# Last stage of a transformer kernel on one core: the gated difference is added into the residual by GpSimd instead of VectorE

## The chip, the cores and the metric

The kernel is one program on one NeuronCore of a Trainium2 chip. Time is device microseconds of that core, and less is better. The engines are TensorE (PE), VectorE (DVE), ScalarE (ACT), GpSimd (POOL) and SyncE (SP), each with its own queue of instructions, and they wait for each other by semaphores that the program sets by hand. Data sits in SBUF, 128 partitions wide; "128x512" is 128 partitions by 512 fp32 elements.

## What is computed

Two pre-norm layers over an input of 4 x 1024 tokens with 128 features: attention, a routed feed-forward, a second attention with fixed offsets, and a last feed-forward with two experts per token. Only the last is touched. Cut to what matters:

```
def _forward(x, ...):
    residual = x
    abel_out = gelu(xn @ abel_w + abel_b)
    topw, topi = top_k(xn @ moe_gate_w + moe_gate_b, 2); topw = softmax(topw)
    moe_out = sum over the two experts of topw * (gelu(xn @ ew1 + eb1) @ ew2 + eb2)
    for i in range(3): moe_out = moe_out @ expm(gens[i])
    gate = sigmoid(concat([abel_out, moe_out]) @ gc_w + gc_b)
    mixed = abel_out * (1.0 - gate) + moe_out * gate
    return residual + mixed
```

The kernel computes the last two lines as residual + abel_out + gate * (moe_out - abel_out). The product with the gate is the "gated difference".

## The kernel before

The residual `x` stays in SBUF for the whole program as 32 tiles of 128 tokens (`[128, 32, 128]`). In the last feed-forward the tokens are sent to their experts' rows in DRAM, 71 tiles of expert rows go through TensorE, and each result row is scattered to `yq` in DRAM by an indirect DMA from POOL (L2132). Beside those tiles, DVE's `pre` steps (L2097 to L2100, one for each of the 32 token tiles) take the gate's share of `ab` (`abel_out`) and add `ab` into `x`.

When all 71 scatters have landed, the part that the change touches begins. The 32 token tiles are taken in eight slices `u` of four tiles. The order of the steps is written out at L1907 to L1913: in turn u come `gate1` of slice u, `mix` of slice u - 1 and `fin` of slice u - 2. Each engine walks that list and does its own part of each step:

- SP loads slice u of `yq` into one of five buffers `yb` (L1947). The first five loads go at once. The later three each wait for the `mix` and the gate sum of the slice whose buffer they take, and stand in SP's queue in turn with the stores (L1951), each of which waits for its slice's `fin`.
- `gate1`: POOL makes the gate's argument in `s0m` with four operations on 128x4 elements (L2142 to L2145), and ACT takes its tanh (L2040).
- `mix`: DVE makes `mo = w0*y0 - ab` (L2111, four operations on 128x128) and `mo = w1*y1 + mo` (L2115, four more), where y0 and y1 are the two experts' rows of `yb`. `mo` has two buffers. POOL turns the tanh into the gate `gt` (L2151). ACT multiplies, `gd = gt * mo` (L2048, four on 128x128). `gd` has two buffers too, so ACT waits for the `fin` of two slices before.
- `fin`: DVE adds `gd` into `x`, one operation on 128x512 (L2121), and signals `v_out`.

`dve.then(ins)` lets DVE wait for its own instruction before the next one. The semaphore names `v_`, `a_`, `g_` and `d_` say who signals: DVE, ACT, POOL or a DMA.

Of the kernel before, what the change touches and what calls it, by code (L numbers as in the profile page):

```python
# [10 lines left out]
ALU = mybir.AluOpType  # L11
# [4 lines left out]
NT = B * T // 128  # L16
# [1785 lines left out]
NX1, NY1, NB1 = 6, 5, 5  # L1802
# [114 lines left out]
def ffn1_sync(p, k, sp, ye):  # L1917
    a = p.a
    ye.dma_start(k.e2T[:], a["e2T"]).then_inc(p.sem("d_f1e").h, 16)
    ye.dma_start(k.b2s[:], a["b2s"]).then_inc(p.sem("d_f1e").h, 16)  # L1920
    ye.dma_start(k.e1[:], a["e1"]).then_inc(p.sem("d_f1e").h, 16)
    sp.wait_ge(p.sem("d_f1"), 16 * len(k.loads))
    ye.dma_start(k.xq[8 * CAP:8 * CAP + 128, :], k.small["pads"][:]).then_inc(p.sem("d_pad").h, 16)
    sp.wait_ge(p.sem("v_end"), 1)
    for e in range(8):
        end = ye.value_load(k.endi[0:1, e:e + 1], min_val=0, max_val=8 * CAP - 128)
        ye.dma_start(k.xq[bass.ds(end, 128), :], k.small["pads"][:]).then_inc(p.sem("d_pad").h, 16)
    sp.wait_ge(p.sem("d_pad"), 16 * 9)
    for q in range(NQ1):
        sp.wait_ge(p.sem(f"d_xq{q}"), 16 * 2 * G * len(range(q, NC1, NQ1)))  # L1930
    sp.wait_ge(p.sem("v_row"), 1)
    for t in range(NE1):
        if t >= NX1:
            sp.wait_ge(p.made("turn1"), t - NX1 + 1)
            sp.wait_ge(p.sem("v_id"), t - NX1 + 1)
        row = ye.value_load(k.rowi[0:1, t:t + 1], min_val=0, max_val=8 * CAP)
        ye.dma_start(k.xg[t % NX1][:], k.xq[bass.ds(row, 128), :]).then_inc(p.sem(f"d_xh{t % NX1}").h, 16)
    for i in range(NY1):
        sp.wait_ge(p.sem(f"d_yq{i}"), 16 * len(range(i, NE1, NY1)))
    o_v = p.out.rearrange("(n p) d -> p n d", p=128)  # L1940
    y_v = k.yq.rearrange("(u p r) d -> u p (r d)", u=8, p=128)
    for u in range(8 + NB1):
        if u < 8:
            if u >= NB1:
                sp.wait_ge(p.sem("v_mo"), u - NB1 + 1)
                sp.wait_ge(p.sem("g_sum"), u - NB1 + 1)
            ye.dma_start(k.y[u % NB1][:].rearrange("p i h d -> p (i h d)"), y_v[u]).then_inc(p.sem(f"d_yb{u % NB1}").h, 16)  # L1947
        if u >= NB1:
            n = 4 * (u - NB1)
            sp.wait_ge(p.sem("v_out"), u - NB1 + 1)  # L1950
            ye.dma_start(o_v[:, n:n + 4, :], p.x[:, n:n + 4, :]).then_inc(p.sem("d_out").h, 16)  # L1951
    sp.wait_ge(p.sem("d_out"), 16 * 8)

# [46 lines left out]
def ffn1_scalar(p, k, act, se):  # L2000
    S = p.S
    cols = k.small["cols"]
    for w in k.items:
        s = w.slot
        if w.kind in R1ACT:
            route1_scalar(p, k.route, act, se, w)
        elif w.kind == "ab":
            c = w.at[0]
            act.wait_ge(p.done("ab"), w.n)
            se.activation(k.ab[:, G * c:G * c + G, :], k.ab[:, G * c:G * c + G, :], ACT.Gelu).then_inc(p.sem("a_ab").h, 1)  # L2010
        elif w.kind == "fold":
            f = w.at[0]
            act.wait_ge(p.made("fold"), w.n)
            se.activation(k.er[:, 774 * f:774 * f + 774].rearrange("p (h n) -> p h n", h=2),
                          S[s][:].rearrange("p (h n) -> p h n", h=2)[:, :, 0:387], ACT.Copy).then_inc(p.done("fold").h, 1)
        elif w.kind == "tiles":
            act.wait_ge(p.sem("v_gap"), NC1)
            se.activation(k.dd[:], k.dd[:], ACT.Tanh, scale=0.5).then_inc(p.sem("a_top").h, 1)
        elif w.kind == "turn1":
            t = w.at[0]  # L2020
            act.wait_ge(p.made("turn1"), w.n)
            if t > 3:
                act.wait_ge(p.made("up1"), t - 3)
            se.activation(k.xT[t % 4][:], S[s][:, 0:128], ACT.Identity, bias=cols[:, 2:3], scale=cols[:, 1:2]).then_inc(p.done("turn1").h, 1)
        elif w.kind == "up1":
            t = w.at[0]
            act.wait_ge(p.made("up1"), w.n)
            act.wait_ge(p.sem("v_w"), w.n)
            if t > 3:
                act.wait_ge(p.made("down1"), t - 3)  # L2030
            for j in range(2):
                c = slice(128 * j, 128 * j + 128)
                ins = se.activation(k.h[t % 4][:, c], S[s][:, c], ACT.Gelu, bias=k.w[t % 4][:, 256 + j:257 + j])  # L2033
            ins.then_inc(p.done("up1").h, 1)
        elif w.kind == "gate1":
            u = w.at[0]
            act.wait_ge(p.sem("g_sum"), u + 1)
            if u == 0:
                act.wait_ge(p.sem("v_half"), 1)
            se.activation(k.s0[u % 2][:], k.s0[u % 2][:], ACT.Tanh, bias=cols[:, 0:1], scale=0.5).then_inc(p.sem("a_gate").h, 1)  # L2040
        elif w.kind == "mix":
            u = w.at[0]
            act.wait_ge(p.sem("v_mo"), u + 1)
            act.wait_ge(p.sem("g_gate"), u + 1)
            if u > 1:
                act.wait_ge(p.sem("v_out"), u - 1)
            for i in range(4):
                ins = se.activation(k.gd[u % 2][:, i, :], k.mo[u % 2][:, i, :], ACT.Identity, scale=k.gt[u % 2][:, i:i + 1])  # L2048
            ins.then_inc(p.sem("a_gd").h, 1)


def ffn1_vector(p, k, dve, ve):
# [9 lines left out]
    for w in k.items:  # L2062
# [21 lines left out]
        elif w.kind == "up1":  # L2084
            t = w.at[0]
            dve.wait_ge(p.sem(f"d_xh{t % NX1}"), 16 * (t // NX1 + 1))
            if t > 7:
                dve.wait_ge(p.sem(f"d_yq{(t - 8) % NY1}"), 16 * ((t - 8) // NY1 + 1))
            ve.tensor_copy(k.id[t % 8][:], k.xg[t % NX1][:, 128:129]).then_inc(p.sem("v_id").h, 1)
        elif w.kind == "down1":  # L2090
            t = w.at[0]
            dve.wait_ge(p.made("down1"), w.n)
            if t >= NY1:
                dve.wait_ge(p.sem(f"d_yq{t % NY1}"), 16 * (t // NY1))
            ve.tensor_tensor(k.yo[t % NY1][:, 0:129], A[s][:, 0:129], k.er[:, bass.ds(expert[t] * 129 + 16 * 129, 129)], ALU.add).then_inc(p.done("down1").h, 1)  # L2095
        elif w.kind == "pre":
            n = w.at[0]  # L2097
            dve.wait_ge(p.sem("a_ab"), n // G + 1)
            ve.tensor_tensor_reduce(k.junk[:], k.ab[:, n, :], sm["gca"][:], 1.0, 0.0, ALU.mult, ALU.add, k.sA[:, n:n + 1])
            dve.then(ve.tensor_tensor(x[:, n, :], x[:, n, :], k.ab[:, n, :], ALU.add))  # L2100
        elif w.kind == "mix":
            u = w.at[0]
            mo, y = k.mo[u % 2], k.y[u % NB1]
            dve.wait_ge(p.sem(f"d_yb{u % NB1}"), 16 * (u // NB1 + 1))
            if u == 0:
                dve.wait_ge(p.sem("a_ab"), NC1)
            if u > 1:
                dve.wait_ge(p.sem("a_gd"), u - 1)
            for i in range(4):
                n = 4 * u + i  # L2110
                ins = ve.scalar_tensor_tensor(mo[:, i, :], y[:, i, 0, 0:128], k.w01[:, 0, n:n + 1], k.ab[:, n, :], ALU.mult, ALU.subtract)  # L2111
            dve.then(ins)
            for i in range(4):
                n = 4 * u + i
                ins = ve.scalar_tensor_tensor(mo[:, i, :], y[:, i, 1, 0:128], k.w01[:, 1, n:n + 1], mo[:, i, :], ALU.mult, ALU.add)  # L2115
            ins.then_inc(p.sem("v_mo").h, 1)
        elif w.kind == "fin":
            u = w.at[0]
            xc = x[:, 4 * u:4 * u + 4, :]
            dve.wait_ge(p.sem("a_gd"), u + 1)  # L2120
            ve.tensor_tensor(xc, xc, k.gd[u % 2][:], ALU.add).then_inc(p.sem("v_out").h, 1)  # L2121


def ffn1_gpsimd(p, k, pool, ge):
    for w in k.items:
# [20 lines left out]
        elif w.kind == "mix":  # L2146
            u = w.at[0]
            pool.wait_ge(p.sem("a_gate"), u + 1)
            if u > 1:
                pool.wait_ge(p.sem("a_gd"), u - 1)  # L2150
            ge.tensor_scalar(k.gt[u % 2][:], k.s0[u % 2][:], 0.5, 0.5, ALU.mult, ALU.add).then_inc(p.sem("g_gate").h, 1)  # L2151

# [2 lines left out]
def program(nc, a, out):  # L2157
# [28 lines left out]
    for i in range(4):  # L2186
        p.again(f"d_yq{i}", f"d_ys{i}", 16 * len(range(i, NE, 4)))
    p.again("d_xq0", "d_sc0", 16 * NT)
    for new, old, n in (("v_id", "a_near", NT), ("v_w", "a_far", NT), ("v_mo", "v_sub", NT), ("g_sum", "v_far", NT), ("v_out", "g_lt", NT),
                        ("a_gd", "v_gate", NCH), ("a_gate", "g_bo", NCH), ("g_gate", "v_add", NT), ("v_pos", "a_ex", 2 * B), ("v_oh", "v_hot", 2 * B),  # L2190
                        ("a_n2", "v_negmax", 2 * B)):
        p.again(new, old, n)
# [165 lines left out]
```

## Time and profile before

| | us |
|---|---|
| median of 3 runs | 1600.14 |
| lowest, highest | 1599.58, 1601.69 |
| the profiled execution's own time | 1601.15 |
| its span in the trace | 1599.4 |
| from `yb` landed (first L2111) to the end of the last L2121 | 1573.11 to 1596.64 |

The profiled execution lies 1.0 us above the median, and 1.75 us of its time lie outside its span. Times in the rows below count from the start of the span. A row of the timeline gives the start, the duration, the engine, the line, the operation, `out<-in` by the program's names (buffer numbers left out), the shapes and how many such instructions are merged in it. The operations of one engine overlap by some tenths of a microsecond at their ends, so four operations of 0.35 us in a row take 1.06 from the first start to the next operation's start.

### The profile page before, as it was taken

How to read it: one execution, taken by the hardware profiler on the slowest of the kernel's cores; microseconds unless marked ns; L12 is line 12 of the kernel's file. 1: busy time of each engine (PE TensorE's matmuls, PEld its weight loads, DVE VectorE, ACT ScalarE, POOL GpSimd, SP SyncE). 2: the span in 40 equal slices, each digit the busy share in tenths (PEclk: the TensorE clock that was granted, in tenths of full speed). 3: DMA queues.
4: the chain of work that ended last, by engine and by line, in shares of the span. 5: the costliest groups of instructions: out<-in, count | busy, mean ns of one | idle time of the engine just before them, and what ended most of it. 6: DMA issues, size and time to landing. Idle time of an engine off the chain costs nothing.

```text
span 1599.4 us, 37167 instructions
## 1 busy us (share of the span) xinstructions
PE 1296.5 (81%) x13212; PEld 850.4 (53%) x13212; DVE 1159.1 (72%) x3814; ACT 728.2 (46%) x1523; POOL 692.9 (43%) x1004
## 2 busy tenths in 40 slices
PE   3479899898998888989896799948999988666881
PEld 2234444445454454544444576627777776556770
DVE  5568788786888969879764554437899998973556
ACT  1136456454565545555561133414544444215773
POOL 3013232233333333323221123347877888764664
PEclk9679999998999999999996799967987777657995
DMA  4664726557264571745705111102111112032335
GB/s 107 93 102 66 117 42 94 81 85 116 31 105 77 91 115 26 115 72 90 112 3 204 56 33 34 41 24 82 43 43 43 49 49 70 21 118 74 92 97 168
DMA packets 73863, 123.19 MB, mean 77 GB/s; under 512 B 17518, under 2 KB 46067, under 8 KB 72784
## 3 DMA queue, kind: packets, MB, share of 16 engines
q1 hardware_dynamic: 64960, 106.74, 35.2%
q0 software_dynamic: 7616, 13.59, 2.6%
q8 instruction: 108, 1.77, 0.5%
q10 hardware_dynamic: 1104, 0.48, 0.1%
q14 instruction: 75, 0.61, 0.1%
HBM read 30.40 MB, written 17.60 MB: 30 GB/s over the span
## 4 chain that ended last, share of the span: by engine, by line
PE 35%; DVE 26%; POOL 12%; SPq 8%; issue 8%; DMA 5%; ACT 4%; DVEq 1%; POOLq 0%; ACTq 0%
SPq L499 8%; DVE first L779 5%; PE S L1033 5%; PE A L593 4%; POOL xq L1356 4%; DVE S L782 3%; PE S L576 3%; PE S L565 3%; PE S L557 2%; PE A L1045 2%; DVE tA L758 2%; POOL prod L1779 2%; PE S L1546 2%; DVE tB L759 2%; PE S L179 1%
## 5 line engine op out<-in xcount | busy, mean ns | idle before, releaser
L670 ACT ACTIVATE P<-S 128x512 f32<-128x512 f32 (+3 forms) x768 | 332.8, 490 | 281.1 <-PE S L576 276.2
L565 PE MATMUL S<-Kp,Qp 120*128 120x512 f32 (+3 forms) x768 | 253.7, 399 | 48.5 <-issue 15.0
L853 POOL TENSOR_SCALAR_AFFINE_SELECT P<-P 128x256 f32<-128x256 f32 (+1 forms) x256 | 116.9, 460 | 403.0 <-ACT P L670 402.7
L576 PE MATMUL S<-Qp,Kp 121*128 121x512 f32 (+3 forms) x768 | 255.1, 396 | 34.4 <-DVE tB L759 9.8
L782 DVE CUSTOM_DVE_ANT_0 S<-S,later 128x512 f32<-128x512 f32 (+3 forms) x512 | 239.2, 514 | 55.4 <-PE S L565 54.8
L565 PEld LDWEIGHTS S<-Kp,Qp 120*128 120x128 f32 x768 | 134.2, 196 | 182.2 <-issue 71.2
L779 DVE TENSOR_REDUCE first<-S 128x1 f32<-128x512 f32 x256 | 164.4, 683 | 49.2 <-PE S L565 49.0
L576 PEld LDWEIGHTS S<-Qp,Kp 121*128 121x128 f32 x768 | 140.0, 193 | 112.5 <-issue 25.2
L593 PE MATMUL A<-P,V 128*9 128x512 f32 (+3 forms) x1536 | 174.0, 501 | 5.6 <-POOL P L853 5.5
L2132 POOL DMA_INDIRECT yq<-yq,id x71 | 69.4, 978 | 48.6 <-DVE yq L2095 26.2
L1779 POOL TENSOR_TENSOR prod<-qf,kT 128x128 f32<-128x128 f32 x160 | 73.3, 492 | 33.1 <-ACT qf L1614 24.8
L1192 POOL DMA_INDIRECT ys<-yo,id x39 | 38.1, 977 | 106.5 <-DVE yo L1172 102.6
L1356 POOL DMA_INDIRECT xq<-n,posu x64 | 67.3, 1052 | 38.1 <-DVE posu L1340 18.8
L1546 PE MATMUL S<-kT,Qm 32*32 32x64 f32 x4096 | 60.2, 234 | 24.1 <-DVE sc L1707 7.6
L1033 PE MATMUL S<-w,xgT 128*128 x156 | 76.5, 613 | 3.6 <-issue 2.2
L1163 DVE SCALAR_TENSOR_TENSOR uu<-th,S 128x512 f32<-128x512 f32 x39 | 26.8, 688 | 68.0 <-ACT th L1065 68.0
L782 DVE DVE_READ_ACCUMULATOR2_ANT mx<- 128x1 f32 x512 | 71.9, 140 | 0.0
L1546 PEld LDWEIGHTS S<-kT,Qm 32*32 32x32 f32 x4096 | 47.8, 109 | 38.5 <-issue 13.1
L1662 ACT ACTIVATE pt<-S 128x1024 f32<-128x1024 f32 x32 | 32.7, 1022 | 55.5 <-PE S L1563 55.5
L758 DVE TENSOR_TENSOR tA<-S,cos 128x512 f32<-128x512 f32 x60 | 41.2, 686 | 21.9 <-PE S L557 11.7
L1995 PE MATMUL A<-er,hq 128*128 x284 | 51.3, 304 | 4.6 <-issue 2.9
L2083 DVE COPY wq<-e 128x258 f32 x71 | 21.5, 302 | 45.4 <-ACT hq L2033 24.8
(335 smaller groups left out, 2707.6 us busy)
## 6 DMA issues: line engine op xcount, KB each, us to landing
Qp<-rcq SPq DMA_DIRECT2D x64, 256.0 KB
Kp<-rck SPq DMA_DIRECT2D x64, 256.0 KB
Qp<-rcq SPq DMA_DIRECT2D x64, 128.0 KB
Kp<-rck SPq DMA_DIRECT2D x64, 128.0 KB
xq<-xq SPq DMA_DIRECT2D x71, 72.0 KB, 1.9
yb<-yq SPq DMA_DIRECT2D x8, 528.0 KB, 4.4
Qp<-cq SPq DMA_DIRECT2D x64, 64.0 KB
Kp<-ck SPq DMA_DIRECT2D x64, 64.0 KB
```

The lines of the kernel that those rows point to most:

```text
L499: ye.dma_start(rows, src).then_inc(p.sem(f"d_q{u % 4}").h, 16)
L565: te.matmul(S[s][:, 512 * h:512 * h + n], Q[0:120, h, 128 * qt:128 * qt + 128], K[0:120, h, 512 * part:512 * part + n], start=True, stop=T ...
L576: te.matmul(S[s][:, 512 * h + c:512 * h + 512], K[0:121, h, 128 * kb:128 * kb + 128], Q[0:121, h, 512 * qh + c:512 * qh + 512], start=True ...
L593: ins = te.matmul(A[oa][o:o + 9, c:512], k.V[u // 8 % 2][:, kb, 2 * (u % 8) + h, :], k.P[(e.n - 1) % NP0][:, h, c:512], start=kb < 2, stop ...
L670: se.activation(k.P[(w.n - 1) % NP0][:, h, c:512], S[s][:, 512 * h + c:512 * h + 512], ACT.Exp, scale=SCALE0).then_inc(p.done("st").h, 1)
L779: ve.tensor_reduce(k.first[:, h, qt - 4:qt - 3], S[s][:, 512 * h:512 * h + 512], AX.X, ALU.max).then_inc(p.done("mx").h, 1)
L782: ins = ve.tensor_tensor_reduce(out=of, in0=of, in1=k.later[:, 512 - n:512], scale=1.0, scalar=-3e38, op0=ALU.add, op1=ALU.max, accum_out= ...
L853: ge.affine_select(P[:, :, start:c + 128], P[:, :, start:c + 128], [[0, 2], [1, wide]], ALU.is_ge, 0.0, base=start - c, channel_multiplier ...
L1033: ins = te.matmul(S[s][:, c:c + 512], k.xgT[t % NH][:], k.w1[:, bass.ds(expert[t] * 1024 + c, 512)], start=True, stop=True)
L1356: ge.indirect_dma_start(r.xq, bass.IndirectOffsetOnAxis(r.posu[q][:, h, i:i + 1], 0), r.n2[q][h][:, i, :], None).then_inc(p.sem(f"d_xq{q}" ...
L1546: ins = te.matmul(C[32 * q:32 * q + 32, 64 * h:64 * h + 64], k.Qm[c % 2][rows, j, 128 * i + 32 * q:128 * i + 32 * q + 32], k.kT[c % 2][row ...
L1779: ins = ge.tensor_tensor(prod[:, n, :], q, kT[:, at:at + 128], ALU.mult)
```

## The change

`fin` moves from DVE's queue to POOL's, at the same place in the list of steps. POOL waits for `a_gd` of the slice and for `v_pre`, a semaphore that now counts DVE's 32 additions of `ab` into `x` (before, DVE counted them on its own semaphore and waited for itself there; it now waits on `v_pre` instead). POOL's addition signals `g_out`, and the three that waited for `v_out` (SP's store, ACT's `gd` buffer, the semaphore's reuse table) take `g_out`.

```diff
@@ ffn1_sync
         if u >= NB1:
             n = 4 * (u - NB1)
-            sp.wait_ge(p.sem("v_out"), u - NB1 + 1)
+            sp.wait_ge(p.sem("g_out"), u - NB1 + 1)
@@ ffn1_scalar
             if u > 1:
-                act.wait_ge(p.sem("v_out"), u - 1)
+                act.wait_ge(p.sem("g_out"), u - 1)
@@ ffn1_vector
-            dve.then(ve.tensor_tensor(x[:, n, :], x[:, n, :], k.ab[:, n, :], ALU.add))
+            ve.tensor_tensor(x[:, n, :], x[:, n, :], k.ab[:, n, :], ALU.add).then_inc(p.sem("v_pre").h, 1)
+            dve.wait_ge(p.sem("v_pre"), n + 1)
...
-        elif w.kind == "fin":
-            u = w.at[0]
-            xc = x[:, 4 * u:4 * u + 4, :]
-            dve.wait_ge(p.sem("a_gd"), u + 1)
-            ve.tensor_tensor(xc, xc, k.gd[u % 2][:], ALU.add).then_inc(p.sem("v_out").h, 1)
@@ ffn1_gpsimd
+        elif w.kind == "fin":
+            u = w.at[0]
+            xc = p.x[:, 4 * u:4 * u + 4, :]
+            pool.wait_ge(p.sem("a_gd"), u + 1)
+            pool.wait_ge(p.sem("v_pre"), NT)
+            ge.tensor_tensor(xc, xc, k.gd[u % 2][:], ALU.add).then_inc(p.sem("g_out").h, 1)
```

DVE's queue in the stage, from the first `mix` of slice 0, before:

```order
3128 L2111 SCALAR_TENSOR_TENSOR mo<-yb,w,ab 128x128 x4
3129 L2115 SCALAR_TENSOR_TENSOR mo<-yb,w,mo 128x128 x4
3130 L2111 SCALAR_TENSOR_TENSOR mo<-yb,w,ab 128x128 x4
3131 L2115 SCALAR_TENSOR_TENSOR mo<-yb,w,mo 128x128 x4
3132 L2121 TENSOR_TENSOR x<-x,gd 128x512
3133 L2111 SCALAR_TENSOR_TENSOR mo<-yb,w,ab 128x128 x4
```

and after it (two lines further down in the file, L2112 is the old L2111, L2116 the old L2115):

```order
3128 L2112 SCALAR_TENSOR_TENSOR mo<-yb,w,ab 128x128 x4
3129 L2116 SCALAR_TENSOR_TENSOR mo<-yb,w,mo 128x128 x4
3130 L2112 SCALAR_TENSOR_TENSOR mo<-yb,w,ab 128x128 x4
3131 L2116 SCALAR_TENSOR_TENSOR mo<-yb,w,mo 128x128 x4
3132 L2112 SCALAR_TENSOR_TENSOR mo<-yb,w,ab 128x128 x4
```

All eight additions are gone from DVE's queue; its `mix` steps of all slices stand in a row.

POOL's queue at the same place, from the `gt` of slice 0 on, before:

```order
586 L2151 TENSOR_SCALAR gt<-s0m 128x4
587 L2142 TENSOR_TENSOR s0m<-yb,w 128x4
588 L2143 TENSOR_TENSOR s1m<-yb,w 128x4
589 L2144 TENSOR_TENSOR s0m<-s0m,s1m 128x4
590 L2145 TENSOR_TENSOR s0m<-s0m,sA 128x4
591 L2151 TENSOR_SCALAR gt<-s0m 128x4
592 L2142 TENSOR_TENSOR s0m<-yb,w 128x4
```

and after it (here the lines are four lower, L2138 is the old L2142 and L2147 the old L2151):

```order
586 L2147 TENSOR_SCALAR gt<-s0m 128x4
587 L2138 TENSOR_TENSOR s0m<-yb,w 128x4
588 L2139 TENSOR_TENSOR s1m<-yb,w 128x4
589 L2140 TENSOR_TENSOR s0m<-s0m,s1m 128x4
590 L2141 TENSOR_TENSOR s0m<-s0m,sA 128x4
591 L2147 TENSOR_SCALAR gt<-s0m 128x4
592 L2153 TENSOR_TENSOR x<-x,gd 128x512
593 L2138 TENSOR_TENSOR s0m<-yb,w 128x4
```

The addition of slice u stands behind the `gt` of slice u + 1 and in front of the four small operations of slice u + 3.

## Rows read from the trace of the kernel before

**Rows 1.** The page's first part: busy time, share of the span, instructions

```profile
PE 1296.5 (81%) x13212; PEld 850.4 (53%) x13212; DVE 1159.1 (72%) x3814; ACT 728.2 (46%) x1523; POOL 692.9 (43%) x1004
```

**Rows 2.** Windows, the last stage: length, then each engine's busy us (instructions), clock, DMA

```profile
1573.00:1597.00 24.00, 0.00 (x0) 0.00 (x0) 22.50 (x72) 12.17 (x40) 11.75 (x40) 0.50 0.66 225
```

**Rows 3.** The chain that ended last, 1569 to the end: start, us, what

```profile
1569.46 3.62 DMA yb<-yq
...
1573.11 1.15 DVE mo L2111 x4
...
1576.51 1.14 DVE mo L2115 x4
1577.65 0.60 DVE x L2121
1578.25 1.06 DVE mo L2111 x4
...
1591.78 0.60 DVE x L2121
1592.38 1.06 DVE mo L2111 x4
...
1593.47 1.15 DVE mo L2115 x4
1594.64 0.40 ACT gd L2048
...
1595.95 0.69 DVE x L2121
```

**Rows 4.** L2121's own view: ns of one, least, median and most; starts; forms

```profile
L2121 DVE TENSOR_TENSOR x<-x,gd x8: 684/684/691, 1577.6 to 1596.0; 128x512 f32<-128x512 f32 x8
```

**Rows 5.** The same view of L1768, POOL's addition in the stage before

```profile
L1768 POOL TENSOR_TENSOR x<-x,bo x8: 1268/1274/1293, 1070.7 to 1295.6; 128x512 f32<-128x512 f32 x8
```

**Rows 6.** L1714's own view, and one L1714 beside POOL's L1768 in the timeline

```profile
L1714 DVE TENSOR_TENSOR sc<-sc,mx x32: 1307/1309/2257, 1085.2 to 1378.4; 128x1104 f32<-128x1104 f32 x32
...
1142.92 1.68 DVE L1714 TENSOR_TENSOR sc<-sc,mx 128x1104 f32<-128x1104 f32 x1
...
1142.15 1.29 POOL L1768 TENSOR_TENSOR x<-x,bo 128x512 f32<-128x512 f32 x1
```

**Rows 7.** L1682's own view, and one L1682 beside POOL's L1791 in the timeline

```profile
L1682 DVE SCALAR_TENSOR_TENSOR x<-yg,share,x x32: 338/350/2110, 1064.6 to 1265.6; 128x128 f32<-128x128 f32 x32
...
1112.89 0.88 DVE L1682 SCALAR_TENSOR_TENSOR x<-yg,share,x 128x128 f32<-128x128 f32 x1
1112.89 0.72 POOL L1791 TENSOR_TENSOR ls<-lt 128x256 f32<-128x256 f32 x1
```

**Rows 8.** Timeline at 1194: POOL's L1791 beside an L1714 that began before it

```profile
1194.03 1.31 DVE L1714 TENSOR_TENSOR sc<-sc,mx 128x1104 f32<-128x1104 f32 x1
...
1194.17 1.75 POOL L1791 TENSOR_TENSOR ls<-lt 128x256 f32<-128x256 f32 x1
```

**Rows 9.** Timeline of the last stage: POOL's small operations, and one L2121 of DVE

```profile
1573.17 0.36 POOL L2142 TENSOR_TENSOR s0m<-yb,w 128x4 f32<-128x4 f32 x1 [4.84 <-DMA yb<-yq]
...
1574.46 0.23 POOL L2142 TENSOR_TENSOR s0m<-yb,w 128x4 f32<-128x4 f32 x1
...
1577.16 0.28 POOL L2151 TENSOR_SCALAR gt<-s0m 128x4 f32<-128x4 f32 x1
...
1577.57 0.69 DVE L2121 TENSOR_TENSOR x<-x,gd 128x512 f32<-128x512 f32 x1
1577.59 0.72 POOL L2142 TENSOR_TENSOR s0m<-yb,w 128x4 f32<-128x4 f32 x1
```

**Rows 10.** DMAs of the last stage, 1569 to the end: count, KB, median us to landing

```profile
yb<-yq SPq DMA_DIRECT2D x8, 528.0 KB, 4.4
out<-x SPq DMA_DIRECT2D x8, 256.0 KB, 2.3
```

More of the change, by code:

```diff
@@ L2188, in program @@
     p.again("d_xq0", "d_sc0", 16 * NT)
-    for new, old, n in (("v_id", "a_near", NT), ("v_w", "a_far", NT), ("v_mo", "v_sub", NT), ("g_sum", "v_far", NT), ("v_out", "g_lt", NT),
+    for new, old, n in (("v_id", "a_near", NT), ("v_w", "a_far", NT), ("v_mo", "v_sub", NT), ("g_sum", "v_far", NT), ("g_out", "g_lt", NT),
                         ("a_gd", "v_gate", NCH), ("a_gate", "g_bo", NCH), ("g_gate", "v_add", NT), ("v_pos", "a_ex", 2 * B), ("v_oh", "v_hot", 2 * B),
```

## The prediction, made before the changed kernel had run

> **What bounds the kernel now.** I read the page's busy shares first: over the whole span VectorE (DVE) is busy 72% and GpSimd (POOL) 43% [rows 1], which says nothing yet about the stage that is changed. The windows view does: in the 24 us from 1573 to 1597 TensorE is idle, DVE is busy 22.50 us, ACT 12.17 and POOL 11.75 [rows 2]. The stage is DVE's. The chain of waits shows how: after the last scatter the read back of `yb` ends at 1573.11, and from there the chain stays on DVE without a gap, four L2111 (1.06), four L2115 (1.14), one L2121 (0.60 by its place in the chain), and so on [rows 3]. L2121 stands in it six times at 0.60, for the slices (u) 0 to 5; the period is 2.82 us (1.06 + 0.02 issue + 1.14 + 0.60). The end is a tail with three members: the last L2115, then ACT's four products (1594.64 to 1595.92), then the last L2121, 0.69 long, then the last store. So six of the eight adds are on the path before the last `mo`, the seventh (u = 6) lies beside ACT's last products, and the eighth closes the kernel.
>
> **What it removes.** Six adds of 0.60 before the last `mo`: 6 x 0.60 = **-3.6 us**. DVE's step falls from 2.82 to 2.22 us, if nothing holds it.
>
> **The last add.** It changes engine. POOL did an add of the same shape, `x<-x,bo`, 128 x 512 in place, eight times, in 1.27 us [rows 5], against DVE's 0.68 to 0.69 [rows 4]: 1.27 - 0.69 = **+0.58 us** (its second input is one row read four times over, which is the one difference). By the Trainium skill (GPSIMD Engine Reference, section 3.1) a two-input op on GpSimd takes about 1.96 times VectorE's time; that would make the last add 1.35 instead of 1.27, and the row is what I use. The store behind it is unchanged, 2.3 us to landing [rows 10].
>
> **The adds in the middle, and what they hold up.** Here is the term that decides. POOL's add of slice u can start when ACT has written `gd`, 1.34 us after the last L2115 of slice u (1594.62 to 1595.95 at the end), and then DVE is in the middle of slice u + 1, in operations that all have two inputs in SBUF (`yb` and `ab`, `yb` and `mo`). The trace of before has many places where such a DVE operation meets a POOL operation that reads SBUF. Four of them:
> - L1714 takes 1.31 alone. At 1142.92 it took 1.68, and POOL's 128 x 512 add was under way from 1142.15 to 1143.44 [rows 6]. It ended 1.16 us after POOL's end: it had waited for POOL to finish and then streamed its 1104 elements.
> - L1682, an operation of the very kind and shape of L2111, takes 0.35 in the median. At 1112.89 it started together with a POOL add of 256 elements (0.72) and took 0.88, ending 0.16 after POOL's end [rows 7]. It was held for 0.88 - 0.35 = 0.53, which is POOL's 0.72 less 0.19.
> - The other way round: at 1194.17 POOL's 256-element add met an L1714 that had begun at 1194.03, and took 1.75 instead of about 0.72. It ended 0.59 after the DVE operation's end [rows 8].
> - In the stage itself POOL's L2142 on four elements began 0.02 after an L2121 and took 0.72, ending at 1578.31, 0.05 after it [rows 9].
>
> So one waits until the other has done its whole operation. POOL's add gets in behind the L2111 or L2115 that is running, and the next one stands until POOL has finished. The price of one add for DVE, as in the L1682 row: 1.27 - 0.19 = 1.08 us. How many meet DVE: the adds of u = 0 to 6 each start 1.3 to 1.4 us into a DVE step that lasts 2.2 or more, so all seven, u = 6 too, which before lay beside ACT and now falls into the last slice's L2115. 7 x 1.08 = **+7.6 us**. Bounds of this price: back-to-back operations start every 0.265 us (1.06 / 4) and stream their 128 elements in 0.13 (L1714's 1104 in 1.16), so up to 0.13 more may be hidden between two, 0.95 each (6.7); or nothing is hidden, 1.27 each (8.9). I take 1.08, since its row is the same DVE instruction. By the Trainium skill (SBUF — State Buffer, "SBUF: two separate sides") the port pair that both engines share is an exclusive lock: whoever starts first has it "for the whole instruction; the other fully blocks". Taken literally that is 1.27 per add and a sum of +5.9 us; the rows bear out that it is exclusive, and price it 0.19 lower.
>
> POOL's four-element operations stand between DVE's now and cost it nothing visible: the step with them (u = 1 to 6) and the last without them both show 1.06 and 1.14 to 1.15 [rows 3]. I leave them at zero.
>
> **What is queued behind the new waits.** On POOL the add waits for `a_gd`. Behind it in POOL's order are the four small operations of slice u + 3 and the `gt` of slice u + 2. A block of four takes 1.29 from start to start, and `gt` 0.3 [rows 9]. So POOL's step is 1.29 + 0.3 + 1.27 = 2.9 us, below DVE's new step of 2.22 + 1.08 = 3.3. `gt` of u + 2 is ready about 1.4 + 1.3 + 1.3 + 0.3 = 4.3 us after slice u's `mo`, and is wanted after two steps, 6.6 us. Cover 2.3 us, cost nothing. On ACT the buffer wait for `gd` is now on slice u - 2's add by POOL, done 4 us earlier. On SP the store of slice 0 stands ahead of the load of `yb` for u = 6. The first add starts when `gt` of u = 1 is written (1577.16 + 0.28) and ends near 1578.8 instead of 1578.26, and a load lands 4.4 us after its issue [rows 9, 10], so near 1583.8; it is wanted at about 1592. Nothing. The wait on `v_pre` (32 signals) is met before the stage: its signals are the old `dve.then` ones under another name, one for one, so it costs neither DVE nor POOL anything.
>
> **The sum.** -3.6 + 7.6 + 0.6 = **+4.6 us**. From the profiled execution, 1601.15 with a span of 1599.4, that gives a span of 1604.0 and a time of 1605.7. That execution lies 1.0 us above the median of the three runs, 1600.14, so as a median **1604.7 us**. With the bounds, -3.6 + 6.7 + 0.6 = +3.7 and -3.6 + 8.9 + 0.6 = +5.9: 1603.8 to 1606.0, and half a microsecond or so more on each side for the median of three runs (they spread over 2.1). A measurement of this kernel can tell about 0.2%, 3.2 us, from no change; the forecast is over that, at 0.29%.
>
> **Rivals.**
> 1. *The add and DVE's operations don't hold each other up* (not slower). Then DVE's last `mo` is 3.6 us earlier and POOL's own queue sets the end: from 1577.44 it has eight adds (10.2), five blocks of four (6.5) and six `gt` (1.8), ending by 1595.9, or up to 1.4 us earlier where its small operations no longer wait for an L2121. Before, the last add ended at 1596.64. That is -0.7 to -2.1, 1598.0 to 1599.4, no change. For it: L2111 is short, with space between two, and POOL's four-element operations go through there unnoticed. Against it: rows 6 to 8, all with long POOL operations. It decides at a price per add below (3.6 - 0.6) / 7 = 0.43 us. Chance 0.10.
> 2. *The blocking is there, but fewer adds meet DVE, or each costs less.* Without the last (u = 6) it is -3.6 + 6 x 0.95 + 0.6 = +2.7, 1602.8. For it: the last add's place in the last slice depends on some tenths. Chance 0.12; two thirds of it lie under 3.2 us.
> 3. *POOL's add gets no turn while DVE has operations in a row* (slower, more). Then each add waits until DVE stops for `a_gd`, nothing overlaps, and the stage is 8 x 2.22 + 8 x 1.27 + 1.3 for ACT = 29.2 from 1573.11, to 1602.3 instead of 1596.6: +5.7, 1605.8. Against it: L2142 was let in at once behind L2121 [rows 9]. Chance 0.07.
> 4. *Something faster by over 3.2 us.* Only if rival 1 holds and POOL's queue is a good deal faster than its rows. Chance 0.03.
>
> **How the numbers follow.** Forecast 0.68, of which almost all is over 3.2 us. Slower by over 0.2%: 0.65 + 0.04 (rival 2) + 0.07 (rival 3) = 0.76. Within 0.2%: 0.10 (rival 1) + 0.08 (rival 2) + 0.03 (the forecast's low end) = 0.21. Faster: 0.03. The range from 1602.3 to 1606.8 holds the forecast with its bounds, rivals 2 and 3, and leaves out rivals 1 and 4 and the rest.
>
> **What would show it.** In the profile after: L2116 (the old L2115) and L2112 with a longest duration near 1.4 us, once in each slice from 1 to 7, each ending 0.15 after a POOL add's end; POOL's adds 1.27 to 1.4 long; DVE's step 3.3 us; the chain alternating between DVE and POOL; the last `mo` near 1598.5 and the last add's end near 1601.2. Right in sign but wrong in its cause: DVE's operations all 0.35 and the end set by POOL's queue. Wrong: DVE's last slice ends near 1591 and the time is under 1600.

## The result: slower, and by twice what was forecast

| | before | changed |
|---|---|---|
| median of 17 runs, us | 1600.9 | 1611.0 |
| lowest, highest | 1595.0, 1605.4 | 1604.2, 1620.6 |
| ratio, 95% interval | | 1.0062 (1.0045 to 1.0078) |
| first `mo` operation to the last `mo` | 21.5 | 24.9 |
| ... to the end of the last addition | 23.5 | 27.6 |
| ... to the end of the span | 26.3 | 36.2 |

The time rose by 10.1 us, 0.62%; forecast were 4.6 us, and 1602.3 to 1606.8. The lower three lines are positions read from the two traces, from the start of the first L2111 (now L2112); the last of them moved by +9.9 us. (Both kernels spread over 10 to 16 us from run to run. The profiled execution of the changed kernel, 1620.6 us, is its slowest. Its first stage, which the change does not touch, already ended 8.2 us later than before; over all the traces of this study VectorE reaches that first barrier between 854.9 and 863.8 us. So positions inside the last stage are compared, not spans. One timed execution of the kernel before, beside e7 and g1, took 1944 us and is left out of the medians there.)

The chain of waits in the last stage (start, us, what), to be held against [rows 3]:

```profile
1582.60 1.15 DVE mo L2112 x4
...
1591.37 1.06 DVE mo L2112 x4
...
1592.46 2.15 DVE mo L2116 x4
...
1602.15 2.15 DVE mo L2116 x4
...
1605.68 1.43 POOL x L2153
1607.11 1.77 issue
1608.88 1.29 POOLq L2196
```

L2121's 0.60 is gone from VectorE's step and four L2116 (the old L2115) take 2.15 instead of 1.14: the step is 3.23 us. That is the blocking, and it has nearly the forecast's size. The own views of the three lines (ns: least, median, most), against [rows 4, 5]:

```profile
L2112 DVE SCALAR_TENSOR_TENSOR mo<-yb,w,ab x32: 334/339/1351, 1582.6 to 1605.0; 128x128 f32<-128x128 f32 x32
...
L2116 DVE SCALAR_TENSOR_TENSOR mo<-yb,w,mo x32: 335/347/1353, 1583.8 to 1607.2; 128x128 f32<-128x128 f32 x32
...
L2153 POOL TENSOR_TENSOR x<-x,gd x8: 1259/1420/1430, 1586.9 to 1608.9; 128x512 f32<-128x512 f32 x8
```

The timeline at the last held operation:

```profile
1605.68 1.43 POOL L2153 TENSOR_TENSOR x<-x,gd 128x512 f32<-128x512 f32 x1 [1.60 <-ACT gd L2048]
1605.91 1.61 DVE L2116 SCALAR_TENSOR_TENSOR mo<-yb,w,mo 128x128 f32<-128x128 f32 x2
...
1608.92 1.26 POOL L2153 TENSOR_TENSOR x<-x,gd 128x512 f32<-128x512 f32 x1 [1.80 <-ACT gd L2048]
```

POOL's addition takes 1.42 where it first waits for the VectorE operation that is running, and 1.26 where VectorE is done. Seven `mo` operations of VectorE are held, each 1.35 long and each ending 0.15 after one of the first seven additions. Two of them are in slice 2 (one L2112, one L2116), and one L2116 in each slice from 3 to 7; slice 1 has none.

The new thing stands behind the last addition, which ends at 1610.18 in a span of 1618.8. SP's waits there, the queue rows of the program's closing line in both kernels (a q behind the engine's name: its sequencer), and POOL's last instruction in the kernel before:

```profile
SPq L2196 <- PEq L2196: 6.1, 1, 6.1
SPq L2196 <- DMA out<-x: 1.9, 1, 1.9
```

```profile
L2196 PEldq DRAIN  x1: 608/608/608, 1573.9 to 1573.9; - x1
L2196 DVEq DRAIN  x1: 2173/2173/2173, 1605.4 to 1605.4; - x1
L2196 ACTq DRAIN  x1: 1306/1306/1306, 1607.6 to 1607.6; - x1
L2196 POOLq DRAIN  x1: 9694/9694/9694, 1608.9 to 1608.9; - x1
```

```profile
L2194 POOLq DRAIN  x1: 8632/8632/8632, 1590.5 to 1590.5; - x1
L2194 ACTq DRAIN  x1: 1304/1304/1304, 1594.7 to 1594.7; - x1
L2194 DVEq DRAIN  x1: 725/725/725, 1596.0 to 1596.0; - x1
...
1590.54 0.19 POOL L2151 TENSOR_SCALAR gt<-s0m 128x4 f32<-128x4 f32 x1 [2.64 <-ACT s0m L2040]
```

Each engine ends the program with a DRAIN, an instruction of its sequencer that starts with the engine's last instructions in these rows and ends behind them, and the span ends behind the last DRAIN. VectorE's and ScalarE's last as long as these engines' last instructions (2.17 and 1.31 us), TensorE's 0.61. POOL's lasts 8.40 us beyond its last instruction: from 1610.18 to 1618.57 in the changed kernel, from 1590.74 to 1599.14 before. SP's wait of 6.1 us is for this (the row names PE, whose DRAIN was over at 1574.5; the one that really came last was POOL). Before, POOL's last instruction was the `gt` of slice 7, and its DRAIN ended at 1599.14, 0.2 us behind the landing of the last store (1598.97). Nothing of it showed: the span ends 0.42 behind that landing, as it does in e6 below, where the DRAIN is over long before. But it had no room left either. Now POOL has the last addition, and 5.9 us of its DRAIN lie bare: POOL's last instruction ends 9.94 us later than before, counted from the first `mo` operation, and the end of the span moves by 9.93.

### The profile page after: what moved, and what is told of

Same layout as the page of the kernel before. It is cut to its first block, busy times and chain, and to the rows that moved or that the text cites. A ratio compares the mean times of both kernels' runs of the same rounds, so it can differ in the third digit from the quotient of the medians.

```text
span 1618.8 us, 37168 instructions
## 1 busy us (share of the span) xinstructions
PE 1299.8 (80%) x13212; PEld 851.1 (53%) x13212; DVE 1163.0 (72%) x3806; ACT 729.1 (45%) x1523; POOL 702.5 (43%) x1012
## 3 DMA queue, kind: packets, MB, share of 16 engines
q0 software_dynamic: 7616, 13.59, 2.6%
## 4 chain that ended last, share of the span: by engine, by line
PE 35%; DVE 29%; POOL 10%; SPq 9%; issue 8%; DMA 5%; ACT 2%; DVEq 1%; POOLq 0%; ACTq 0%
SPq L499 8%; DVE first L779 5%; PE S L1033 4%; PE A L593 4%; DVE S L782 4%; PE S L576 3%; PE S L565 3%; POOL xq L1356 3%; PE S L557 2%; PE A L1045 2%; DVE tA L758 2%; POOL prod L1779 1%; DMA xq<-xq 1%; PE A L1995 1%; DVE tB L759 1%
## 5 line engine op out<-in xcount | busy, mean ns | idle before, releaser
L1652 ACT ACTIVATE pr<-sc 128x1024 f32<-128x1024 f32 x32 | 34.3, 1071 | 44.4 <-DVE sc L1714 44.3
```

## Experiments

The theory after this result has two parts. **A:** an addition on POOL and a VectorE operation with both inputs in SBUF exclude each other, for most of the length of the addition; and POOL's DRAIN has a long tail that only shows when POOL works last. **A1:** this tail grows with the number of DMAs that POOL has issued since its last DRAIN. The rivals: long additions on POOL bring the long end themselves; the tail is fixed; the hold is a fixed price of each meeting. All positions in this table are us from the first `mo` operation, read from the timelines; the last column is POOL's closing DRAIN beyond POOL's last instruction.

| kernel | last `mo` | last addition | end of span | DRAIN's tail |
|---|---|---|---|---|
| before | 21.49 | 23.53 | 26.27 | 8.40 |
| changed | 24.92 | 27.57 | 36.20 | 8.40 |
| e1, POOL last | 21.49 | 23.53 | 32.42 | 8.38 |
| e2, one DRAIN before the scatters | 24.95 | 27.60 | 33.70 | 5.87 |
| e3, four additions on each engine | 23.14 | 25.18 | 27.91 | 8.40 |
| e4, half-wide additions | 21.17 | 23.28 | 31.91 | 8.40 |
| e5, `mo` through PSUM | 19.42 | 22.08 | 30.71 | 8.40 |
| e6, three DRAINs | 24.96 | 27.61 | 30.34 | 0.97 |
| g1, best of both | 19.43 | 21.47 | 24.21 | 2.93 |

### e1 and e7: one small operation on POOL, at the very end

```diff
+    pool.wait_ge(p.sem("v_out"), 8)
+    ge.tensor_scalar(k.s1[0][:], k.s1[0][:], 0.5, 0.5, ALU.mult, ALU.add)
```

> The kernel before, with one more GpSimd operation on 128x4 elements (s1m, used by nobody any more) that waits for the last addition of VectorE. Theory A, the end of the program: GpSimd's closing DRAIN takes 8.4 us after that engine's last instruction (8.40 in both traces), and in the changed kernel it only becomes visible because GpSimd works last. Then the stage up to the last addition stays at 23.5 us from the first L2111, and from there to the end of the span come 0.05 + 0.2 + 8.40 + 0.24 = 8.9 us instead of 2.8: 32.4 us in all instead of 26.3, and the time is +6.1 us (+0.38%). Theory B, the extra time at the end comes from GpSimd's long additions themselves or from blocked stores: 26.3 us and no change in time (within 0.05%).

The end of e1's timeline, whose span is 1638.6:

```profile
1629.06 0.69 DVE L2121 TENSOR_TENSOR x<-x,gd 128x512 f32<-128x512 f32 x1 [0.74 <-ACT gd L2048]
...
1629.84 0.19 POOL L2153 TENSOR_SCALAR s1m<-s1m 128x4 f32<-128x4 f32 x1 [5.99 <-DVE x L2121]
```

and its closing DRAIN, in the view of that line:

```profile
L2196 POOLq DRAIN  x1: 8617/8617/8617, 1629.8 to 1629.8; - x1
```

All the additions are on VectorE, where they were, and one operation of 0.19 us on 128x4 elements moves the end by 6.15 us: 32.42 as expected. So the long end needs no long addition. The times showed less of it, 1.0010 (0.9983 to 1.0037), and I timed the same kernel again:

> The same kernel as e1_pool_last, timed in five rounds, because there the trace showed the 6.1 us and the times +0.10% with an interval of 0.27 to each side. Theory A: 32.4 us from the first L2111 to the end of the span, and +0.2 to +0.5% in the times (6.1 us are 0.38%). Theory B, that this end lies outside what the times measure: 0.0 to 0.1%.

1.0005 (0.9980 to 1.0031), again with 32.42 in the trace. Neither interval reaches the 1.0038 that the trace asks for, and the second time came out as theory B has it. That was the one result against the theory, and it is taken up below (r1, r2).

### e2 and e6: a DRAIN earlier on POOL

```diff
             t = w.at[0]
+            if t == 0:            # e6: t in (0, 36, 60)
+                ge.drain()
             pool.wait_ge(p.done("down1"), w.n)
```

> The changed kernel with a DRAIN added on GpSimd in front of the first of the 71 scatters, where GpSimd is idle for 12.7 us anyway. Theory A1, a DRAIN's length follows the number of DMAs that GpSimd has issued since the last one (4.67 us after 56, 8.40 after 103, 2.75 after 32 in the traces of before and after: 0.19 + 0.080 each): the added one takes some 2.7 us, costs nothing, and the closing one falls to 0.19 + 71 x 0.080 = 5.9 us. From the first L2112 to the end of the span 33.7 us instead of 36.2. Theory A2, the closing DRAIN has a fixed length of 8.4 us, whatever stands before it: 36.2 us.

> The changed kernel with three DRAINs on GpSimd: before the first, the 37th and the 61st of the 71 scatters. Theory A1 (0.19 + 0.080 us per DMA since the last DRAIN): the closing DRAIN stands behind 11 DMAs, lasts 1.1 us after GpSimd's last instruction and hides behind the last store; the end follows the last addition by 2.8 us, 30.4 us after the first L2112 instead of 36.2, which leaves only the blocking's +4.1. The two in the middle take 3.1 and 2.1 us and may hold the scatters up by as much. Theory A2 (what is waited for is something else, as the landing of the last scatters): 33.7 as with one DRAIN, or more.

The last addition in e2's timeline, and its closing DRAIN in the view of that line:

```profile
1628.46 1.26 POOL L2155 TENSOR_TENSOR x<-x,gd 128x512 f32<-128x512 f32 x1 [1.80 <-ACT gd L2048]
```

```profile
L2198 POOLq DRAIN  x1: 7164/7164/7164, 1628.4 to 1628.4; - x1
```

The same two of e6, with the last store:

```profile
1603.52 1.26 POOL L2155 TENSOR_TENSOR x<-x,gd 128x512 f32<-128x512 f32 x1 [1.80 <-ACT gd L2048]
1604.81 0.37 SPq L1951 DMA_DIRECT2D out<-x  x1
```

```profile
L2198 POOLq DRAIN  x1: 2264/2264/2264, 1603.5 to 1603.5; - x1
```

e6's three added DRAINs, and the packets of all of POOL's DMAs on the page of before:

```profile
L2127 POOLq DRAIN  x3: 3669/4447/17847, 1437.0 to 1554.0; - x3
```

```profile
q0 software_dynamic: 7616, 13.59, 2.6%
```

Nothing in the stage changed, and the end moved by 2.5 and 5.9 us, as the count says. Over the traces, the tail beyond POOL's last instruction against the DMAs issued since the DRAIN before it: 11: 0.97; 24: 2.21; 32: 2.75 (and 2.62 in e2); 35: 2.93; 36: 2.99; 56: 4.67; 71: 5.87; 103: 8.40. A line of 0.19 + 0.080 each goes through them within 0.13. With e6's three DRAINs only the stage's own loss is left, 30.34 against 26.27. The 56 of the first stage hold 32 direct DMAs and 24 indirect ones and lie on the same line, so the kind makes no difference here. Whether it is the DMAs that are counted or their packets is not told apart: the program's 238 DMAs from POOL make 7616 packets, 32 for each.

The two DRAINs among the scatters were not free. The 71 scatters took 106.7 us from first to last in e6, against 102.2 and 102.3 in f1 and e5, which ran on the same chip: 4.4 us lost ahead of the stage, for 3.4 more won at the end than with e2's single DRAIN.

### e3: the blocking without the late POOL

```diff
-        elif w.kind == "fin":                      # on POOL
+        elif w.kind == "fin" and w.at[0] < 4:      # on POOL
...
+        elif w.kind == "fin" and w.at[0] >= 4:     # on VectorE, as before
```

> The changed kernel with the additions of slices 0 to 3 on GpSimd and those of 4 to 7 on VectorE, so that GpSimd's last instruction is early again. It shows the blocking alone. Theory A (blocking of 1.0 us per addition beside VectorE, and a closing DRAIN that shows only when GpSimd works last): the stage up to the last addition takes 23.5 - 4 x 0.60 + 4 x 1.01 = 25.2 us, and the end follows 2.8 us later, 28.0 us in all (+1.7). Theory B (long GpSimd additions bring a long end wherever they stand): 25.2 + 8.6 = 33.8 us.

25.18 to the last addition and 27.91 to the end. Four additions of 1.3 to 1.4 on POOL, and no long end. The tail of 8.40 is there as before, but POOL's last instruction is the `gt` of slice 7 again, and its DRAIN ends at 1629.36, 0.18 behind the landing of the last store.

### e4 and e5: what a hold costs, and what it needs

```diff
-            ge.tensor_tensor(xc, xc, k.gd[u % 2][:], ALU.add)
+            ge.tensor_tensor(xc[:, 0:2, :], xc[:, 0:2, :], k.gd[u % 2][:, 0:2, :], ALU.add)
```

> The changed kernel with GpSimd adding only the first two of the four token tiles of each slice (128x256 in place of 128x512; the addition of the other two is left out). Theory A, VectorE stands for as long as GpSimd's operation lasts, less 0.2 to 0.26: GpSimd's addition takes 0.72 and holds VectorE for some 0.46 instead of 1.01 us, seven times; four L2116 with one hold in them take 1.6 instead of 2.15 us; the stage up to the last addition is 27.6 - 7 x 0.55 - 0.55 = 23.2 us. Theory B, the hold is a fixed price of each handover between the two engines: the groups stay at 2.15 us and the stage at 27.0 us.

e4 leaves half of the additions out; it serves only to measure the hold. The last held group in e4's chain, and the own views of its two lines:

```profile
1617.32 1.62 DVE mo L2116 x4
```

```profile
L2116 DVE SCALAR_TENSOR_TENSOR mo<-yb,w,mo x32: 337/348/812, 1601.6 to 1621.3; 128x128 f32<-128x128 f32 x32
...
L2153 POOL TENSOR_TENSOR x<-x,gd x8: 722/884/887, 1604.8 to 1623.0; 128x256 f32<-128x256 f32 x8
```

Half the addition (0.72 alone instead of 1.26) cuts the longest L2116 from 1.35 to 0.81, by the same 0.54. The hold follows the addition's length; it is no fixed price. In both cases it is the addition less 0.26 (1.26 and 1.00, 0.72 and 0.46).

```diff
-    ve.scalar_tensor_tensor(mo[:, i, :], y0, w0, k.ab[:, n, :], ALU.mult, ALU.subtract)
+    ve.scalar_tensor_tensor(half[:, i, :], y0, w0, k.ab[:, n, :], ALU.mult, ALU.subtract)   # half: PSUM
-    ve.scalar_tensor_tensor(mo[:, i, :], y1, w1, mo[:, i, :], ALU.mult, ALU.add)
+    ve.scalar_tensor_tensor(mo[:, i, :], y1, w1, half[:, i, :], ALU.mult, ALU.add)
```

> The changed kernel with the first half of mo written to PSUM and read from there by the second four operations (the old L2115), which so have one input in SBUF and one in PSUM; all else as in the changed kernel. Theory A, the two engines exclude each other only where VectorE's operation has both inputs in SBUF: GpSimd's additions start 1.3 to 1.4 us into each step, where the second four operations now run freely. No operation of them is longer than 0.6 us, four take 1.1 to 1.5 us instead of 2.15, GpSimd's additions take 1.27, and the last addition ends 22 to 25 us after the first L2112 instead of 27.6 (VectorE's 8 x 2.3 to 2.6 or GpSimd's own queue of 2.9 a step). Theory B, a GpSimd addition stops any VectorE operation: holds of 1.0 us stay, the stage takes 27.6 or more.

The own views of its two `mo` lines and of POOL's addition:

```profile
L2113 DVE SCALAR_TENSOR_TENSOR S<-yb,w,ab x32: 346/348/1059, 1575.5 to 1593.4; 128x128 f32<-128x128 f32 x32
...
L2117 DVE SCALAR_TENSOR_TENSOR mo<-yb,w,S x32: 342/342/349, 1576.7 to 1594.6; 128x128 f32<-128x128 f32 x32
...
L2154 POOL TENSOR_TENSOR x<-x,gd x8: 1261/1262/1265, 1579.6 to 1596.3; 128x512 f32<-128x512 f32 x8
```

and the timeline at slice 7:

```profile
1591.54 1.26 POOL L2154 TENSOR_TENSOR x<-x,gd 128x512 f32<-128x512 f32 x1
...
1592.43 1.32 DVE L2113 SCALAR_TENSOR_TENSOR S<-yb,w,ab 128x128 f32<-128x128 f32 x4
...
1593.79 1.12 DVE L2117 SCALAR_TENSOR_TENSOR mo<-yb,w,S 128x128 f32<-128x128 f32 x4
1593.91 1.26 POOL L2154 TENSOR_TENSOR x<-x,gd 128x512 f32<-128x512 f32 x1 [0.90 <-ACT gd L2048]
```

The lower two lie over each other almost whole, and neither is longer for it: 0.342 to 0.349 for all 32 operations of L2117, 1.26 for all eight additions. L2113 still has both inputs in SBUF (it writes to PSUM), and it is held: the first L2113 of each slice from 2 to 7 ends 0.15 to 0.16 after an addition, having taken 1.06 once and 0.53 to 0.54 five times, where only the addition's end falls into it. So the condition is both inputs in SBUF, not the engine pair as such. The Trainium skill (SBUF — State Buffer, "SBUF: two separate sides") states this condition, and the runs agree; that a meeting costs VectorE the addition's whole length they do not show: 1.00 for 1.26.

### r1 and r2: are the DRAIN's microseconds in the times?

> The changed kernel itself, timed beside the next one on one chip. In the traces its end lies 36.2 us after the first mo operation against 26.3 before: +9.9 us. If the times follow the traces: +0.6%. If the closing DRAIN (5.9 us of it) were not in the times, as e1 and e7 (+0.10% and +0.05% where the trace has 6.1 us) let one suspect: +4.1 us, +0.25%.

> The kernel of e3_four_and_four (additions 0 to 3 on GpSimd, 4 to 7 on VectorE), timed. The trace has +1.65 us against before, +0.1%, and 8.3 us less than the changed kernel. If the times follow the traces, the two kernels of this call lie 0.5% apart; if the closing DRAIN is not in the times, only 0.15%.

On one chip: the changed kernel 1642.2 us, 1.0042 (1.0015 to 1.0068); e3's kernel 1633.2 us, 1.0007 (0.9980 to 1.0034). They lie 8.9 us apart by the medians, where the traces have 8.2 (36.21 against 27.97) and only 2.3 without the DRAIN. With the first comparison's +10.1 for a trace's +9.9 that speaks for the DRAIN being in the times. The profiled executions settle it. Each has a time and a span, the span ends behind the DRAIN, and the time is 1.75 to 1.84 us longer than the span in all 14 traces, whether the DRAIN lies bare (changed 1620.56 and 1618.81, e1 1640.39 and 1638.64) or is hidden (before 1601.15 and 1599.39, e3 1631.35 and 1629.60). If it were not in the times, e1's would be some 6 us shorter. So theory B of e7 is out. What stays open is why the medians of e1 and e7 moved by 2.0 and 1.5 only: their stage shows the full 6.15 in both traces, and what their other executions did ahead of it is not on record. The executions of one kernel spread over some 15 us, but two intervals that both end short of the value are not comfortable.

### f1 and f2: DRAINs where the barrier waits for POOL

The program has three barriers at which the engines wait for each other, each with a DRAIN on L861. The same tail stands at the one behind the first feed-forward, before the change and after: before, VectorE reaches it at 1049.4, and POOL's DRAIN of 3.89 us ends at 1058.8.

```diff
# f1, at the head of the loop over 39 tiles
+        if t in (0, 13, 25, 35):
+            ge.drain()
# f2, behind the tile's small copy and before the wait for its scatter
+        if t == 12:
+            ge.drain()
```

> The kernel before, with four DRAINs added on GpSimd in the first feed-forward (before scatters 0, 13, 25 and 35 of 39), where GpSimd is idle for some 2 us in every 3.2. Theory A1: the DRAIN at the barrier behind it stands behind 4 DMAs instead of 47 and takes 0.5 instead of 3.9 us; all engines wait for it there, so 3.4 us less (-0.2%). From the end of VectorE's DRAIN at that barrier to the end of GpSimd's 6.1 us instead of 9.5. If the added DRAINs (1.2 us each) hold up the scatters, some of it is lost again. Theory A2 (a fixed length, or the landing of the last scatters): no change.

> The kernel before, with a single DRAIN in the first feed-forward, behind the small copy of tile 12 and in front of the wait for its scatter, where GpSimd idles 6.7 us. Theory A1: it takes under 3 us, holds nothing up (the step from scatter 11 to 12 stays at 8.6 to 8.7 us), and the DRAIN at the barrier stands behind 27 DMAs: 0.19 + 27 x 0.080 = 2.35 us instead of 3.89. Theory A2 (no count): 3.9 us.

The barrier's POOL DRAINs of before, f1 and f2, of three barriers each; the one in question is the least:

```profile
L861 POOLq DRAIN  x3: 3887/3937/5117, 844.9 to 1397.9; - x3
```

```profile
L861 POOLq DRAIN  x3: 371/3937/5118, 847.7 to 1403.6; - x3
```

```profile
L861 POOLq DRAIN  x3: 2249/3939/5120, 847.5 to 1400.2; - x3
```

The count held again, 0.37 behind 4 DMAs and 2.25 behind 27 (0.51 and 2.35 by the line). But f1 was slower, 1.0044 (1.0015 to 1.0072). Its timeline on POOL, at the added DRAIN before tile 13:

```profile
974.11 0.97 POOL L1194 DMA_INDIRECT ys<-yo,id  x1 [7.53 <-DVE yo L1172]
977.08 0.18 POOL L1191 CAST id<-xg 128x1 uint32<-128x1 f32 x1 [1.99 <-issue]
978.04 0.97 POOL L1194 DMA_INDIRECT ys<-yo,id  x1 [0.78 <-POOL id L1191]
```

f1's four added DRAINs end 1.44, 1.85, 1.97 and 1.61 us after POOL's last instruction, behind 8, 13, 12 and 10 DMAs: 0.6 to 0.8 more than the line. Standing straight behind a DMA is not the reason by itself, for the DRAINs of e6 and g1 straight behind a scatter, with 24 and 36 DMAs, show nothing of the kind (2.21 and 2.99), and behind 20, as f2's, it is 1.93 where the line has 1.79. That a DRAIN also waits for the last DMA still under way, which would show only where the count is small, would fit (where a landing is on record, it comes 1.3 us after the issuing instruction's end), but it was not tested.

Behind the second of them the small copy comes 2 us late. SP's next load of `xg` waits for that copy (for 9.5 us at the longest in this stretch, where it was 7.5 before), TensorE waits 1.4 us for the load, and POOL then stands 5.56 us for VectorE's `yo`. The three steps from scatter to scatter that follow the DRAIN take 3.93, 2.73 and 6.73 us, where they took 3.59, 3.16 and 3.16, so 3.5 us are lost, and 2.1 more behind the DRAIN before tile 25. From the end of VectorE's DRAIN at the first barrier to the end of POOL's at the second, f1 takes 205.3 us, against 202.5 before and 203.1 and 203.9 in e5 and e6, which ran on the same chip: a net loss of 1.4 to 2.9 us. The interval begins at 2.4 us, and what the rest is stays open. I had priced the DRAIN by its count alone and put it in a gap that it does not fit. f2's single one, behind the copy in a gap of 7 us, held nothing up that could be seen (scatter 11 to 12: 8.97, before 8.64; all 39 took 133.1 us, before 133.5) and took 1.6 us off the barrier.

### g1: what is left when both costs are out

e5's `mo` through PSUM, the addition of slice 7 alone on VectorE, DRAINs on POOL before scatters 0 and 36 of the 71, and f2's.

> The changed kernel with the cheap parts kept and the two costs taken out: the first half of mo goes through PSUM (no holds), the addition of slice 7 alone is back on VectorE (0.69 instead of 1.26), GpSimd gets a DRAIN before scatters 0 and 36 of the 71 (35 DMAs are left for the closing one: 0.19 + 2.8 = 3.0 us after GpSimd's last instruction, hidden behind the last store), and one in the first feed-forward, in the idle 6.7 us before scatter 12 of 39. Theory A: last mo 19.4 us after the first mo operation, last addition 21.5, end of the span 24.2 instead of the 26.3 of the kernel before (-2.1 us); the barrier behind the first feed-forward comes 1.5 us sooner after its last scatter. Together -3.6 us, -0.2%, less what the DRAIN before scatter 36 holds up (up to 3 us). Theory B, the closing DRAIN is not set by the number of DMAs: the end 29 to 31 us after the first mo operation, slower than before.

Its chain at the end, and its closing DRAIN in the view of that line:

```profile
1630.85 1.13 DVE mo L2119 x4
...
1633.32 0.69 DVE x L2124
```

```profile
L2205 POOLq DRAIN  x1: 4232/4232/4232, 1630.9 to 1630.9; - x1
```

24.21 us to the end instead of 26.27, the barrier 1.6 us earlier, and 0.9958 (0.9934 to 0.9982) in the times, 6.4 us by the medians: faster than the kernel before. The traces account for 3.7 us of it, less what the DRAIN before scatter 36 costs: there the step from scatter to scatter took 4.83 us instead of 1.49, and the 71 scatters took 127.2 us from first to last, against 125.1 and 125.3 in e7 and f2, which ran on the same chip, so some 2 us. -3.7 us (0.9977) lies just inside the interval, and the net -1.7 (0.9990) outside it. So that g1 is faster is measured, but the traces do not explain all of it. Its parts were not timed one by one.

## Why the prediction was wrong

- **The sign and the mechanism in the stage were right.** The forecast was slower, by seven of POOL's additions each holding up one `mo` operation of VectorE that ends 0.15 after the addition. So it is. One detail was off: not one in each slice from 1 to 7. The addition of slice 0 waits for POOL's `gt` and starts 4.3 us after the first `mo` operation (the prediction's own part on POOL's queue has it there), at the very end of slice 1's step, so slice 2 has two holds and slice 1 none. The number of seven stands.
- **The stage's own terms held.** Removed: 6 x 0.60 = 3.6, as forecast. Holds: the last `mo` came 3.43 later, so the seven cost 3.43 + 3.6 = 7.0 instead of 7.6; 1.00 each, not 1.08, within the stated 0.95 to 1.27. L1682 in [rows 7] had begun together with POOL's operation; in a row of operations POOL gets in between two, and the 0.26 that is hidden is about the 0.265 at which they follow each other. That is a reading, not a test. The literal reading of the Trainium skill's lock, 1.27 each, is farther off. Last addition: +0.61 against +0.58. Together +4.04 against +4.6; e6 shows this sum by itself (30.34 against 26.27). Counted from the first L2111 at 1573.11, the last `mo` ends at 1598.0 and the last addition at 1600.7, where 1598.5 and 1601.2 were forecast. The chain does not alternate between VectorE and POOL, as the forecast had it; it stays on VectorE up to the last slice.
- **The step that failed is the tail**, "The store behind it is unchanged". It is, but the store is not what the program ends with. The sum followed the last addition to its store and stopped there; what POOL does after its last instruction was in no term and no rival. It is worth 5.9 us, more than all the rest: 4.0 + 5.9 = 9.9, the traces' difference, and the times' 10.1. The row was there: POOL's closing DRAIN of 8632 ns at 1590.5 in the trace of before, ending at 1599.14 of 1599.4. The part "What is queued behind the new waits" went through POOL's queue only up to the last slice.
- **The range** was made of the sizes of the terms that were in the sum. A term that is not in it cannot widen it.
- **The rivals.** No blocking (0.10): ruled out by e4 and the changed trace, though e5 shows what it would look like: 22.1 us to the last addition. With it goes POOL's queue as the bound: POOL idled 1.6 and 1.8 us before the last two additions. Fewer meetings or cheaper ones (0.12): all seven met, at 1.00 instead of 1.08. No turn for POOL (0.07): ruled out; its additions were 0.17 us longer at most. Something faster (0.03): not so.
- `v_pre`, the `yb` loads and the order of the queues cost nothing, as forecast: the stage's sum closes without them.

## What to carry to other kernels

Before an operation is moved to GpSimd, ask what it meets on VectorE: here it cost a VectorE that worked without a gap, on operations with both inputs in SBUF, its own length less 0.26 us, while an operand in PSUM let the two run side by side. Then ask what the engine has to do after its last instruction: follow a moved last operation beyond its store, to every engine's closing DRAIN, which the page does not list and the queue rows of the closing line do. Where GpSimd issues many DMAs, its DRAINs at barriers and at the end are work of their own. An earlier DRAIN in an idle stretch takes it off the path (e2, f2); in a busy one it costs some of it again (e6, g1) or more than it wins (f1).

## What the hardware showed that was not expected

- A DRAIN on GpSimd ends 0.19 us and 0.080 us for each DMA that it has issued since the DRAIN before (of 32 packets each) after its last instruction, measured behind 11 to 103 DMAs; that is 8.4 us at the end of this kernel.
- Behind 8 to 13 DMAs of which the last had just been issued it took 0.6 to 0.8 us more than that (1.85 behind 13); behind 24 and 36 it did not.
- The last stage repeats from run to run and from chip to chip to within 0.1 us (21.49, 23.53, 26.27 for the same code), while the first, of 855 us, varies by 9. The 71 scatters take 102 to 107 us from first to last in five of the 14 traces (the three of one chip among them) and 121 to 127 in the other nine.
